# Layer 0 of a four-layer graph kernel: two row tiles' products with the node weights in one run, and half of an adjacency product between the runs

## The reference, cut to what matters

```
As = [eye, A, 2 A A - eye]                       # K = 3
w  = einsum('nd,dkio->nkio', embedding, weight)  # d = 16: a 64 x 64 matrix of each node and k
x_g = einsum('knm,bmc->bnkc', stack(As), x)
out = einsum('bnki,nkio->bno', x_g, w) + b
x = layernorm(x + out)
...
layer 1: x = layernorm(x + elu(softmax attention over adj > 0.5, which is nowhere met: a mean over all nodes))
layer 2: x = layernorm(x + (adj + eye) (x W + b) / degree)
layer 3: three steps of v = relu([v, adj v] W1 + b1) W2 + b2, then x = layernorm(x + v)
```

## Time and profile before

| what | value |
|---|---|
| median of 3 runs | 1030.81 us (1030.46 to 1031.53) |
| span of the profiled execution | 1029.5 us |
| the profiled execution's own time | not in the results apart from the three runs; its span is 1.3 us under their median |
| PE busy | 1009.6 us (98%) |
| DVE busy | 678.8 us (66%) |
| POOL busy | 553.4 us (54%) |
| ACT busy | 457.4 us (44%) |
| MIDDLE in the trace | from the first Z at 108.1 us to the end of the last at 523.2 us |

### The profile page before, as it was taken

One profiled execution on the slowest core, in us unless ns is written; L12 is line 12 of the kernel. 1 busy time (PEld: TensorE's weight loads), 2 busy tenths in 40 slices (PEclk: granted clock), 3 DMA queues, 4 the chain that ended last, 5 costly groups with the idle time before them and its releaser, 6 DMA issues.

```text
span 1029.5 us, 18650 instructions
## 1 busy us (share of the span) xinstructions
PE 1009.6 (98%) x6854; PEld 485.6 (47%) x6854; DVE 678.8 (66%) x1683; ACT 457.4 (44%) x1109; POOL 553.4 (54%) x645
## 2 busy tenths in 40 slices
PE   7999999999999999999999999999999999999995
PEld 3445444444444444434445556555555545455553
DVE  3886565666566786578567767886663646657556
ACT  4632323453345445543543454432556655232632
POOL 0004487776658698879878465474534233323311
PEclk9999999999999999999999999999999999999998
DMA  9930000000000000000010111000033231000022
GB/s 375 402 136 1 1 1 2 1 2 1 1 1 2 1 2 2 1 2 1 1 42 1 41 42 42 2 1 1 3 122 108 98 123 42 4 2 21 21 62 62
DMA packets 14658, 45.65 MB, mean 44 GB/s; under 512 B 960, under 2 KB 9280, under 8 KB 10080
## 3 DMA queue, kind: packets, MB, share of 16 engines
q1 hardware_dynamic: 14560, 44.39, 11.7%
HBM read 40.19 MB, written 4.19 MB: 43 GB/s over the span
## 4 chain that ended last, share of the span: by engine, by line
PE 90%; DVE 6%; ACT 2%; issue 1%; POOL 0%; DMA 0%; SPq 0%; ACTq 0%; DVEq 0%; POOLq 0%
PE PS L962 28%; PE PS L925 23%; PE PS L795 22%; PE PS L847 5%; PE PS L780 2%; PE PS L781 2%; PE PS L782 2%; ACT WZ L1075 1%; DVE X L1543 1%; DVE X L1231 1%; PE PS L789 1%; PE PS L787 1%; PE PS L788 1%; DVE T L1231 1%; PE PS L770 1%
## 5 line engine op out<-in xcount | busy, mean ns | idle before, releaser
L795 PE MATMUL PS<-BW,S 128*128 128x512 fp8e4 x1280 | 290.7, 379 | 0.7 <-DVE R L1231 0.7
L1075 ACT ACTIVATE T<-PS,SM 128x128 f32<-128x128 f32 x384 | 113.2, 366 | 203.8 <-DVE X L1231 135.8
L925 PE MATMUL PS<-WZ,R 64*128 64x512 f16 x1536 | 197.8, 377 | 0.0
L795 PEld LDWEIGHTS PS<-BW,S 128*128 128x128 f16 x1280 | 120.2, 98 | 149.4 <-issue 16.6
L962 PE MATMUL PS<-BW,S 128*128 128x512 fp8e4 x768 | 173.1, 379 | 0.1
L1749 POOL TENSOR_TENSOR T<-T 128x128 f32<-128x128 f32 (+1 forms) x192 | 124.3, 647 | 79.8 <-ACT T L1075 61.8
L1231 DVE SCALAR_TENSOR_TENSOR X<-PS,SM,X 128x128 f32<-128x128 f32 x320 | 109.9, 344 | 76.0 <-PE PS L925 75.9
L925 PEld LDWEIGHTS PS<-WZ,R 64*128 64x128 f16 x1536 | 69.5, 94 | 102.6 <-issue 26.3
L962 PEld LDWEIGHTS PS<-BW,S 128*128 128x128 f16 x768 | 73.8, 98 | 83.4 <-issue 0.6
L962 PE MATMUL PS<-BW,T 128*128 128x512 fp8e4 x480 | 109.3, 379 | 0.0
L1749 POOL TENSOR_TENSOR S<-R,S 128x512 f16<-128x512 f32 (+1 forms) x46 | 52.5, 1148 | 103.9 <-ACT S L1075 103.9
(11 more groups left out here) (210 smaller groups left out, 1496.6 us busy)
## 6 DMA issues: line engine op xcount, KB each, us to landing
WZ<-a_in SPq DMA_DIRECT2D x16, 1024.0 KB, 4.8
BW<-at_in SPq DMA_DIRECT2D x8, 1024.0 KB, 18.9
R<-at_in SPq DMA_DIRECT2D x7, 1024.0 KB, 12.9
out<-X SPq DMA_DIRECT2D x16, 256.0 KB, 2.3
X<-x_in SPq DMA_DIRECT2D x3, 1024.0 KB, 20.6
T<-w_in SPq DMA_DIRECT2D x1, 1536.0 KB, 16.1
R<-at_in SPq DMA_DIRECT2D x2, 512.0 KB, 4.1
SM<-sm_in SPq DMA_DIRECT2D x1, 520.5 KB, 18.9
```

The lines of the kernel that those rows point to most:

```text
L795: m = e.matmul(o, stile(h, t, c), Bm[:, t, block(j)], start=(t == 0 and h == 0), stop=(last and t == NT - 1 and h == 1))
L925: m = e.matmul(bank(b0 + q), halves[kd][zh][r, :], WZ[r, wh, kd, block(g)], start=(i == 0), stop=(i == 8))
L1075: return e.activation(o, i, f, **kw)
```

## The change

```diff
-        each = len([x for x in beside if x[0][0] == "P"]) // 4
-        for t in range(4):
+        each = len([x for x in beside if x[0][0] == "P"]) // 2
+        for t in (0, 2):
+            turned = ("dx", "t1") if c < 3 and j < 2 else ()
+            v = 4 * (c + 1) + 2 * j + t // 2
+            order += [(x, v) for x in turned[:1]]
             n = 0
             while beside and (n < each or beside[0][0][0] == "E"):
                 n += beside[0][0][0] == "P"
                 order.append(beside.pop(0))
-            order += [("Z", u, t), ("add", u, t)]
-            order += after.pop(4 * u + t, [])
-            if c < 3 and j < 2:
-                v = 4 * (c + 1) + 2 * j + t // 2
-                order.append(("dx" if t % 2 == 0 else "t1", v))
+            order += [(x, v) for x in turned[1:]]
+            for i in (t, t + 1):
+                order += [("Z", u, i), ("add", u, i)]
+                order += after.pop(4 * u + i, [])
```

## The result

The changed kernel takes 1042.2 us (1041.97 to 1042.63, 4 runs), against 1031.17 us for the kernel before beside it (4 runs): ratio 1.0107, 95% interval 1.0095 to 1.0119. That is 11.0 us slower. The forecast was 1037.2 us, 6.4 us slower, with a range up to 1042.5. Direction and mechanism were right, the size was not: 4.6 of the 11.0 us were not forecast.

The account below looks back on a forecast made before the run. PE, busy 98% of the span, was taken to bound the kernel. New waits of 15.4 us less a gain of 9.0 (6.7 hand-overs, 2.3 old waits) gave +6.4, so 1037.2 us, own range 1033.6 to 1040.6, stated range 1032.0 to 1042.5.

Parts of the forecast that it names:

- the gain at the hand-overs: MIDDLE: 32 runs of Z instead of 64 save 32 x 0.21 = 6.7 us, with no gap between adjacent Z.
- t1 too close behind dx: Both write bank 1; only half a product lies between, so t1, due 3.9 us after h, waits for dx's eviction.
- t1(9): After row tile 17: no chk ahead, bank free 3.8 us after h against 3.9, so no wait.
- t1(8), t1(12) and t1(13): After row tiles 15, 31 and 33: ACT's queue ahead of dx makes PE wait 1.7, 2.2 and 1.35 us.
- t1(15): After row tiles 36 and 37, norm stretch: 3.4 us wait, between 1.7 unstretched and 4.75 with DVE stretched beside GpSimd.
- dx(4): First step of MIDDLE: waits 1.6 us for bank 1, just filled by HEAD's last P1.
- E1(12): Now ahead of row tile 4: ACT waits for xs(3) on POOL, PE loses 1.45 us (1.2 to 1.6) at row tile 5.
- There no t1 is made: Row tile 54, behind the second norm stretch: only bank reuse priced, 0.5 us (0 to 1.45).
- third rival: Evictions of two Z come in a burst; six other pairs wait about 1 us each, giving 1043 us; chance 0.14.
- so nothing is made up: Behind MIDDLE everything starts later by the same amount, since PE's waits there follow its own earlier work.
- rival of no change: Norm-stretch waits and row tile 54 cost 0.3 us together, giving 1031.0 us; chance 0.08.
- faster one: ACT and DVE reach dx within half a product's cover, leaving only a 1.6 us wait: 1023.4 us; chance 0.10.

Follow-up runs that it names:

- e1_t1_behind: Changed kernel with dx directly ahead of the two Z and t1 directly behind the pair: 1031.06 us, ratio 1.0004 to the kernel before.
- e2_chk_earlier: Changed kernel with chk of chunks 0 and 1 one pair earlier, so none stands ahead of dx(8) and dx(12): 1038.38 us.
- e8_other_bank: Changed kernel with the last P1 of HEAD in bank 2, so that dx(4) finds bank 1 free: 1041.56 us.
- e4_units_8_9: Kernel before, with the new grouping only in units 8 and 9 of sixteen: 1040.8 us, ratio 1.0098.
- e5_behind_p2_first: Changed kernel with the edits of e1_t1_behind and e3_p2_first together: 1027.18 us, ratio 0.9962 to the kernel before.
- e7_less_gpsimd: e5_behind_p2_first with one GpSimd adjacency subtraction (1.1 us) moved from behind row tile 54 to later: 1026.03 us, ratio 0.9951 to the kernel before.
- e3_p2_first: Changed kernel with P2(2) ahead of P1(4) in unit 1, so ACT reaches E1(12) a pair later: 1041.26 us.
- e6_pairs_alone: Changed kernel with only the pairing kept: dx behind a pair's first Z, t1 behind its second, as before: 1034.67 us, ratio 1.0030.

## Why the prediction was right, and where it fell short

**Right: the gain at the hand-overs.** 0.21 us a pair, and none inside a run of 72: it takes 7.88 us, which is 36 slots of 0.216 and one hand-over of 0.1.

**Right: t1 too close behind dx.** Six of the seven t1 that it priced came out within 0.1 us, t1(9)'s nothing among them. t1(8), t1(12) and t1(13) could be read off the trace before: the end of the last ACT instruction ahead of dx, plus 1.4, less the 3.9 that PE takes. e1_t1_behind (all gone) and e2_chk_earlier (one gone and one down to 0.35 with what stood ahead) show the cause. t1(15) was mis-sized, 3.4 against 2.62. The rs was stretched less than in the earlier trace rows: one of its five small instructions took 0.98 us in place of 0.19, not three of them. It and GpSimd's adds beside it:

```profile
373.89 2.66 POOL L1751 TENSOR_TENSOR T<-T 128x384 f32<-128x384 f32 x3 [3.57 <-ACT T L1077]
...
373.95 0.98 DVE L1533 TENSOR_TENSOR T<-T 128x32 f32<-128x32 f32 x1
```

The two-input DVE instruction starts 0.06 us behind the first of the three adds and ends 0.05 us behind that add's end. This agrees with the rule of the Trainium skill (SBUF — State Buffer, "Who interferes with whom"). But the 4.75 us that the prediction worked out by the rule was not met: it took all of today's stretching to come again, and it came in full for one instruction.

**Right: dx(4) and E1(12)**, 1.58 and 1.71 for 1.6 and 1.45. E1(12)'s lies above its stated bounds of 1.2 to 1.6, since PE came for the banks at 146.46 and not at 146.7; the end of xs(3) was right by two offsetting errors (e8_other_bank).

**Short: the sum had no term for the clock.** "New waits: ... = 15.4 us" took a wait as worth its length. Two of 2.5 us cost another 1.7 each, 3.4 in all. It is the largest part of what is missing. That it isn't the pairs is shown by e4_units_8_9 (the same falls, no pairs in 14 units) and by e5_behind_p2_first and e7_less_gpsimd (pairs everywhere, no wait over 2 us in layer 0, no fall in the trace, and 0.995 to 0.997 in all ten executions). All falls seen in layer 0 stand directly behind waits of over 2 us; what decides which of these bring one stays open.

**Short: "There no t1 is made", behind the second norm stretch.** I looked there for reuse of banks and for P2, and not for the mean, which takes GpSimd's sum. POOL's queue in the changed kernel, with the same columns:

```profile
460.11 2.39 POOL L1751 TENSOR_TENSOR T<-T 128x384 f32<-128x384 f32 x3 [2.86 <-ACT T L1077]
...
494.89 2.61 POOL L1751 TENSOR_TENSOR SM<-SM,X 128x512 f32<-128x512 f32 x2
```

Between the two nothing is idle: 37 us of adds, splits, one bt and the sum, for three pairs and a mean that PE does in less. The pair from 466.44 to 479.05 alone takes GpSimd 12.6 us, where PE needs 11.44. The third rival had named such saturation at 11.0 us of 11.4, with two addrow; it came with two addrow and two splits, and cost 1.6 us at one place, not 1 us in each of six pairs. That the sum on GpSimd holds the mean up is shown by e7_less_gpsimd for a wait of 0.5 us; for the 1.6 us here it is read off the rows.

**Short: "so nothing is made up" was right, that nothing is added was not.** In TAIL a wait at line 782 grew from 0.9 to 1.65 us. It is 1.63 to 1.66 in every kernel with pairs throughout and 0.84 in e4_units_8_9. What it hangs on stays open: no experiment was aimed at it.

**Luck: the range held.** The forecast's own range ended at 1040.6. Its ends were also added up wrongly: the low and high ends as stated give 11.05 and 19.25 us, not 11.8 and 18.8, so 1032.9 to 1041.1. The 1042.5 came from the upper half of the third rival, whose mechanism did not occur: no wait in six further pairs, only at row tiles 5 and 55. What filled that room was mostly the clock.

The rival of no change wanted t1(14), t1(15) and row tile 54 to cost 0.3 us together; they cost 2.69 + 2.62 + 0.29 = 5.6. The faster one wanted ACT and DVE to get to dx within 3.9 us; six t1 waited, 11.0 us in all.

## What to carry to other kernels

- When two steps share a buffer, what counts is not only the work between them but what the evicting engines have in their queues ahead of the first. A regrouping that adds nothing to the bound engine can still put every other engine's work between the two. Here dx and t1 turned around the pair, with one product swapped, made a gain of 0.4% of a loss of 1.1%.
- Read such a wait off the old trace: end of the last instruction ahead, plus the eviction, less the cover. It was good to 0.1 us at five t1 that wait, and off by 0.8 us at t1(15), where DVE and GpSimd meet.
- Look through every producer of an operand in the stretch that gets denser, also those off the path, and price a wait of over 2 us on PE with the clock that it may cost.

## What the hardware showed unexpectedly

- The granted clock fell from 2.4 to 1.2 GHz for about 3.4 us behind PE waits of 2.1 to 3.3 us, and cost 1.7 us each time. It fell behind 2.53 and 2.46 in the changed kernel and not behind its 2.08; in e3_p2_first it fell behind 2.07 and 2.52 and not behind 2.46. At row tile 5, between two Z, 3.05 us (e1_t1_behind) and 2.35 us (e8_other_bank) brought no fall in the profiled executions; six other executions of e1_t1_behind have a lower mean clock (0.993 or 0.994) than any of the kernel before. Waits of up to 2.0 us (e6_pairs_alone) brought none in layer 0. In e2_chk_earlier a wait of 3.27 us cost the same 1.7 as one of 2.53.
- A hand-over to paired 64-row matmuls and back costs 0.21 us of PE (11.65 before against 11.44 us a pair), in layer 0's MIDDLE.
- A DVE instruction of 128x32 with two inputs in SBUF took 0.98 us in place of 0.19 beside a GpSimd add, and ended 0.05 us behind it.
